# The second layer's graph-attention loop, run one step deeper

## The reference, cut to what matters

```
h = relu(layernorm(x))
score   = h @ H_v                                    # one number for each node
logits  = where(adj != 0, adj * score[None, :], -1e30)
weights = softmax(logits, axis=-1)
x = x + weights @ h
```

## Time and profile before

| | before |
|---|---|
| median of 3 runs | 1568.05 us (1566.85 to 1569.98) |
| profiled execution | 1554.0 us |
| its span | 1552.3 us |
| TensorE products, busy | 1006.1 us (65% of the span) |
| VectorE, busy | 895.8 us |
| GpSimd, busy | 768.8 us |
| ScalarE, busy | 756.1 us |
| bytes moved | 219.73 MB, 142 GB/s on average |

### The profile page before, as it was taken

The page is one execution under the profiler, slowest core; times in us unless marked ns, Lnnn a source line. Parts: engine busy times, 40 slices in busy tenths (PEclk is TensorE's granted clock), DMA queues, the critical chain, the costliest instruction groups (busy, mean ns, idle before and its releaser), DMA issues.

```text
span 1552.3 us, 29120 instructions
## 1 busy us (share of the span) xinstructions
PE 1006.1 (65%) x6426; PEld 631.8 (41%) x6426; DVE 895.8 (58%) x2430; ACT 756.1 (49%) x3228; POOL 768.8 (50%) x791
## 2 busy tenths in 40 slices
PE   4696858888974515545554286981746777777770
PEld 1353524544542314434443243441524554555440
DVE  3494855986886235544555750103436777777778
ACT  4997666678741313323333250000625666676762
POOL 3007766764555256555655505665054555555550
PEclk9797979898986556665766688996868999999995
DMA  8546656874512444554445876855242445333462
GB/s 272 194 192 227 223 182 180 257 230 166 208 40 64 122 129 101 104 100 94 109 104 98 95 245 224 301 186 62 82 134 79 106 97 105 97 105 100 101 89 58
DMA packets 124455, 219.73 MB, mean 142 GB/s; under 512 B 37350, under 2 KB 93290, under 8 KB 118762
## 3 DMA queue, kind: packets, MB, share of 16 engines
q0 software_dynamic: 25984, 60.45, 21.8%
q1 hardware_dynamic: 83050, 74.24, 15.4%
q10 hardware_dynamic: 15360, 84.43, 14.3%
HBM read 182.18 MB, written 33.18 MB: 139 GB/s over the span
## 4 chain that ended last, share of the span: by engine, by line
DVE 30%; issue 22%; PE 18%; another core or an unknown queue 13%; DVEq 6%; ACT 3%; DMA 3%; SPq 1%; ACTq 1%
DVE work L1380 4%; DVE work L1114 4%; PE ps L1673 3%; PE ps L1716 3%; DVE work L1115 2%; PE ps L1725 2%; PE ps L1526 2%; DVEq L418 1%; DVE work L1051 1%; DVE work L1048 1%; DVE work L1396 1%; DVEq L322 1%; DMA work<-adj_table 1%; PE ps L1522 1%
## 5 line engine op out<-in xcount | busy, mean ns | idle before, releaser
L685 POOL DMA_INDIRECT work<-h_table,stage x304 | 290.6, 956 | 258.8 <-issue 124.9
L801 ACT ACTIVATE unread<-work 128x128 bf16<-128x128 f32 x1024 | 301.0, 295 | 40.8 <-DVE work L1119 16.5
L685 POOL DMA_INDIRECT work<-kv_table,stage x212 | 201.5, 951 | 222.3 <-PE ps L1735 120.5
L642 POOL DMA_INDIRECT work<-in_adj_rows,adj_stage x184 | 238.4, 1296 | 82.6 <-issue 57.0
L1568 PE MATMUL ps<-work,h_wide 128*128 128x512 f32 x512 | 248.5, 641 | 25.5 <-ACT h_wide L732 18.3
L801 ACT ACTIVATION_READ_ACCUMULATOR unread<-work 128x1 f32 x1024 | 191.5, 187 | 7.3 <-issue 6.9
L1380 DVE CUSTOM_DVE_ANT_0 work<-ps,work 128x512 f32<-128x512 f32 x200 | 141.7, 748 | 76.5 <-remote 40.9
L1568 PEld LDWEIGHTS ps<-work,h_wide 128*128 128x128 f32 x512 | 103.7, 208 | 153.7 <-issue 144.8
L1725 PE MATMUL ps<-ident,work 128*128 128x128 f32 x776 | 116.9, 284 | 43.5 <-DVE work L1396 25.1
L893 ACT ACTIVATE work<-work 128x512 f32<-128x512 f32 x197 | 139.8, 713 | 3.5 <-DVE work L1389 2.9
L1648 PE MATMUL ps<-work 128*128 128x128 f32 x384 | 85.9, 394 | 68.9 <-ACT work L842 52.3
(11 more groups left out here) (216 smaller groups left out, 1802.4 us busy)
## 6 DMA issues: line engine op xcount, KB each, us to landing
work<-in_adj_rows ACTq DMA_DIRECT2D x38, 2048.0 KB
work<-adj_table SPq DMA_DIRECT2D x76, 256.0 KB
work<-in_adj_rows SPq DMA_DIRECT2D x6, 2048.0 KB
adj_table<-work SPq DMA_DIRECT2D x96, 128.0 KB
mask_table<-work SPq DMA_DIRECT2D x53, 128.0 KB
work<-mask_table SPq DMA_DIRECT2D x53, 128.0 KB
work<-h_table,stage POOLq DMA_INDIRECT x304
kv_table<-work SPq DMA_DIRECT2D x32, 128.0 KB
```

Source lines behind the costliest of these rows:

```text
L642: nc.gpsimd.indirect_dma_start(out=ag[:, h, c, :], out_offset=None, in_=adj_rows, in_offset=bass.IndirectOffsetOnAxis(ap=adj_stage[:, h // ...
L685: nc.gpsimd.indirect_dma_start(out=rows[:, b, c, :], out_offset=None, in_=table, in_offset=bass.IndirectOffsetOnAxis(ap=stage[:, b, c:c + ...
L801: ins = nc.scalar.activation(unread[:, m % (MQ // 2) * TB + t, :], ring[:, q, m, t * P:(t + 1) * P], ACT.Abs, accum_out=seen[:, b, t, q * ...
```

## The change

The loop's order is changed on three engines; no operation of a group is added or taken away.

- VectorE makes logits four groups ahead instead of two and before the maximum, takes the maximum two groups ahead instead of one, and adds up group g as before.
- The transposed logits and their source `lgT` have three buffers instead of two (PSUM banks 0, 1 and 2).
- TensorE, in step g, transposes the exponentials of g+1, multiplies those of g, and then transposes the logits of g+3.
- ScalarE, in step g, copies the transposed exponentials of g+1 and makes exponentials and mask of g+2. The copies, `eT`, have two buffers.
- The parts ahead of the loops, the waits' constants and the primed semaphores follow. SP's and GpSimd's orders stay; the semaphores that they wait for (`lgT_ready`, `mk_ready`) now come from earlier steps, and after the loop SP waits for one more mask.

```diff
--- before.py
+++ after.py
@@ -175,7 +175,7 @@
         hg2 = work[:, 2048:4096].rearrange("p (b c f) -> p b c f", b=NBUF2, c=QC)
         kvg = work[:, 0:6144].rearrange("p (b c f) -> p b c f", b=NBUF, c=QC)
         neg = work[:, 6168:6680]
-        lgT = work[:, 6680:7704].rearrange("p (b c n) -> p b c n", b=2, c=QC)
+        lgT = work[:, 6680:8216].rearrange("p (b c n) -> p b c n", b=3, c=QC)
         e = work[:, 8704:12800].rearrange("p (b h m) -> p b h m", b=2, h=H)
         e1 = e[:, :, 0, :]
         eT = work[:, 12800:14848].rearrange("p (c h n) -> p c h n", c=QC, h=H)
@@ -299,6 +299,7 @@
                   oT_out, o_done, lgT_ready, lg_done, cap_ready, eT_outd, mk_ready, mk_ready] + [mk_free] * NBUF
         for k in (1, 2, 3):
             primed += [pv_done[k], pv_done[k], pv_read[k], pv_read[k], state_reset[k]]
+        primed += [pv_read[1], pv_read[1]]
         for k in (1, 3):
             primed += [mx_ready[k], e_ready[k], e_ready[k], al_ready[k], eT_done[k], eT_out[k]]
 
@@ -540,7 +541,7 @@
                 steps = sparse_quads(sp, step) if k == 2 else each_quad(sp, step)
                 if k == 1:
                     end = Quad(steps, 0)
-                    sp.wait_ge(mk_ready, end.q + 3)
+                    sp.wait_ge(mk_ready, end.q + 4)
                     for n in range(NBUF - 1):
                         sp.dma_start(mask_table[bass.ds((end.q + n) * P, P), :], mk[:, 0, :]).then_inc(mk_all, 16)
                     sp.wait_ge(mk_all, 16 * (NBUF - 1))
@@ -827,30 +828,33 @@
                 act.wait_ge(eT_done[1], q + 1)
                 act.wait_ge(pv_read[1], q + 1)
                 nc.scalar.activation(alpha[:, b:b + 1], grown[:, b:b + 1], ACT.Exp).then_inc(al_ready[1], 1)
-                nc.scalar.activation(e1[:, b % 2, :], ps[:, b % 2, :], ACT.Exp, bias=nbest[:, b:b + 1],
+                nc.scalar.activation(e1[:, b % 2, :], ps[:, b % 3, :], ACT.Exp, bias=nbest[:, b:b + 1],
                                      accum_out=part[:, b:b + 1]).then_inc(e_ready[1], 1)
 
             def mask1(g):
 
                 act.wait_ge(mk_free, g.q + 1)
-                nc.scalar.activation(mk[:, g.b, :], ps[:, g.b % 2, :], ACT.Relu, bias=half_neg[:, 0:1],
+                nc.scalar.activation(mk[:, g.b, :], ps[:, g.b % 3, :], ACT.Relu, bias=half_neg[:, 0:1],
                                      scale=-1.0).then_inc(mk_ready, 1)
 
             def turned1(g):
                 act.wait_ge(eT_done[1], g.q + 2)
-                act.wait_ge(pv_done[1], g.q + 2)
-                nc.scalar.activation(eT[:, :, 0, :], ps[:, 3, :].rearrange("p (c n) -> p c n", c=QC),
+                act.wait_ge(pv_done[1], g.q + 1)
+                nc.scalar.activation(eT[:, :, g.b % 2, :], ps[:, 3, :].rearrange("p (c n) -> p c n", c=QC),
                                      ACT.Copy).then_inc(eT_out[1], 1)
 
             def step1(g):
-                turned1(g)
-                exps1(g.ahead(1))
-                mask1(g.ahead(1))
+                turned1(g.ahead(1))
+                exps1(g.ahead(2))
+                mask1(g.ahead(2))
 
             use_exp()
             act.wait_ge(tables_ready, 1)
             exps1(Quad(0, 0))
             mask1(Quad(0, 0))
+            turned1(Quad(0, 0))
+            exps1(Quad(0, 1))
+            mask1(Quad(0, 1))
             each_quad(act, step1)
 
             normalise(2)
@@ -1226,13 +1230,13 @@
                 adj_loaded(dve, 1, g)
                 nodes_gathered(dve, 1, g)
                 dve.wait_ge(lgT_ready, q + 1)
-                wait(dve, lg_done, q)
+                wait(dve, lg_done, q - 1)
                 link = Link(dve, link_a, 1, q)
                 link(nc.vector.tensor_scalar(neg, ac[:, b, :, :].rearrange("p c n -> p (c n)"), 0.0, NEG,
                                              ALU.is_equal, ALU.mult))
                 link.end()
                 for c in range(QC):
-                    ins = nc.vector.scalar_tensor_tensor(lgT[:, b % 2, c, :], ac[:, b, c, :], hg1[:, b, c, P:P + 1],
+                    ins = nc.vector.scalar_tensor_tensor(lgT[:, b % 3, c, :], ac[:, b, c, :], hg1[:, b, c, P:P + 1],
                                                          neg[:, c * P:(c + 1) * P], ALU.mult, ALU.add)
                 ins.then_inc(lgT_ready, 1)
 
@@ -1243,7 +1247,7 @@
                 capped = cap[:, bass.ds(q, 1)]
                 dve.wait_ge(lg_done, q + 2)
                 link = Link(dve, link_m, 2, q)
-                link(nc.vector.tensor_reduce(want, ps[:, b % 2, :], AX.X, ALU.max))
+                link(nc.vector.tensor_reduce(want, ps[:, b % 3, :], AX.X, ALU.max))
                 link(nc.vector.scalar_tensor_tensor(best[:, b:b + 1], old, capped, want, ALU.min, ALU.max))
                 link.end()
                 nc.vector.scalar_tensor_tensor(grown[:, b:b + 1], old, capped, best[:, b:b + 1], ALU.min, ALU.subtract)
@@ -1262,7 +1266,7 @@
                 settle(dve)
                 nc.vector.scalar_tensor_tensor(acc[:, t, :], acc[:, t, :], alpha[:, b:b + 1], ps[:, 4 + b % 4, 0:P], ALU.mult,
                                                ALU.add).then_inc(pv_read[1], 1)
-                dve.wait_ge(pv_read[1], q + 3)
+                dve.wait_ge(pv_read[1], q + 5)
                 settle(dve)
 
             def finish1():
@@ -1284,8 +1288,8 @@
                 link.end()
 
             def step1(g):
-                maxima(g.ahead(1))
-                logits(g.ahead(2))
+                logits(g.ahead(4))
+                maxima(g.ahead(2))
                 add_up(g)
 
             dve.wait_ge(mean_done, T + 1)
@@ -1297,11 +1301,17 @@
                                   .to_broadcast([P, T + 1, P])).then_inc(state_reset[1], 1)
             dve.wait_ge(state_reset[1], 2)
             logits(Quad(0, 0))
+            logits(Quad(0, 1))
             maxima(Quad(0, 0))
-            logits(Quad(0, 1))
+            logits(Quad(0, 2))
+            maxima(Quad(0, 1))
+            logits(Quad(0, 3))
             end = Quad(each_quad(dve, step1), 0)
 
-            dve.wait_ge(e_ready[1], end.q + 3)
+            dve.wait_ge(e_ready[1], end.q + 4)
+            dve.wait_ge(eT_out[1], end.q + 2)
+            dve.wait_ge(lg_done, end.q + 4)
+            dve.wait_ge(mk_ready, end.q + 4)
             settle(dve)
             finish1()
             dve.wait_ge(stat_done2, 1)
@@ -1628,27 +1638,37 @@
             def logits(g):
                 q, b = g.q, g.b
                 pe.wait_ge(lgT_ready, q + 2)
-                pe.wait_ge(mk_ready, q + 1)
+                wait(pe, mk_ready, q)
                 for c in range(QC):
-                    ins = nc.tensor.transpose(ps[:, b % 2, c * P:(c + 1) * P], lgT[:, b % 2, c, :], ident[:, :])
+                    ins = nc.tensor.transpose(ps[:, b % 3, c * P:(c + 1) * P], lgT[:, b % 3, c, :], ident[:, :])
                 ins.then_inc(lg_done, 1)
 
-            def step1(g):
+            def turn_exps1(g):
                 q, b = g.q, g.b
                 pe.wait_ge(e_ready[1], q + 3)
                 pe.wait_ge(eT_out[1], q + 1)
                 for c in range(QC):
                     ins = nc.tensor.transpose(ps[:, 3, c * P:(c + 1) * P], e1[:, b % 2, c * P:(c + 1) * P], ident[:, :])
                 ins.then_inc(eT_done[1], 1)
-                logits(g.ahead(1))
+
+            def weigh1(g):
+                q, b = g.q, g.b
                 pe.wait_ge(eT_out[1], q + 2)
                 pe.wait_ge(pv_read[1], q + 1)
                 nodes_gathered(pe, 1, g)
                 for c in range(QC):
-                    ins = mm(ps[:, 4 + b % 4, 0:P], eT[:, c, 0, :], hg1[:, b, c, 0:P], start=(c == 0), stop=(c == QC - 1))
+                    ins = mm(ps[:, 4 + b % 4, 0:P], eT[:, c, b % 2, :], hg1[:, b, c, 0:P], start=(c == 0), stop=(c == QC - 1))
                 ins.then_inc(pv_done[1], 1)
 
+            def step1(g):
+                turn_exps1(g.ahead(1))
+                weigh1(g)
+                logits(g.ahead(3))
+
             logits(Quad(0, 0))
+            logits(Quad(0, 1))
+            turn_exps1(Quad(0, 0))
+            logits(Quad(0, 2))
             each_quad(pe, step1)
 
             project(2)
```

## The result

The changed kernel takes 1587.82 us (median of 4 runs, 1582.98 to 1589.87), the kernel before beside it 1569.01 us. The ratio is 1.0113, 95% interval 1.0081 to 1.0145: slower by 1.1%, 18.8 us between the medians. Forecast was 1556.3 us and faster. The time lies inside the range given, on the side of the slower rival, but far from that rival's 1603 us.

What follows compares the result with a forecast made beforehand. The second layer's loop was taken as bound by a two-group cycle of gathers and held TensorE results, 12.3 us. SP's queue -10.1, Start +4.7 and End -6.4 sum to -11.8: 1568.05 becomes 1556.3 us; whole range 1536 to 1598.

Steps and rivals of the forecast that it cites:

- slower rival: Second layer's loop: gathers come too late, pace 7.28 us a step, +35.3 us with the start, 1603 us; chance 0.30.
- End: After the second layer's loop: SP reaches its last masks and lists one step earlier, third layer's first gather too; -6.4 us.
- DMA path to 942.06: After the loop: from SP's 2 MB loads at 896.04 us to the third layer's first gather at 942.06.
- The gathers' slack: Loop: logits two steps earlier leave gathers two steps of four; costs 0, with 2.4 us to spare over three steps.
- The ring of 16.0 us: Loop: gather, landing, logits, maximum, exponential, transposes, sums, to the next gather; 16.0 us for three steps, 5.3 a step.
- The pattern of 7.28 us a group: Fourth layer's loop, where one group is gathered and then waited for; the slower rival takes its 7.28 us as pace.
- SP's queue: Loop: logits and mask come earlier, so GpSimd's waits for SP's loads shrink from 19.7 us to 0; -10.1 us.
- no change: Loop: GpSimd's permission and cycle stay, SP's gain returns as longer holds, or held time is TensorE's; 1568 us, chance 0.16.
- Start: Loop's start: group 0's sums now also stand behind the weights of group 1; +4.7 us.
- Signals: Loop: longer distance from logits' transposes to maximum; two groups still get through per run of gathers; 0.
- much faster: Loop: late results have a cause independent of gathers, depth hides holds, 5.0 us a step; 1515 us, chance 0.12.

Runs made afterwards that it cites:

- e13: Kernel before with unused list places naming 128 different rows instead of one, on a chip of the second kind: 1335.82 us, ratio 0.9896.
- e14: Changed kernel with unused list places naming 128 different rows instead of one, on a chip of the second kind: ratio 1.0016.
- e9: Kernel before with the second layer's indirect gathers replaced by plain DMAs of 128 consecutive rows, on a chip of the first kind: 1477.61 us, ratio 0.9425.
- e12: Changed kernel with logits three groups ahead, behind the maximum, on a chip of the second kind: 1356.94 us, ratio 1.0067.
- e19: Changed kernel with logits three groups ahead, behind the maximum, and unused list places naming 128 different rows, on a chip of the first kind: ratio 1.0037.
- e15: Changed kernel with logits three groups ahead, behind the maximum, and unused list places naming 128 different rows, on a chip of the second kind: ratio 0.9977.
- e16: Changed kernel, unaltered, on a chip of the second kind: 1382.02 us, ratio 1.0251 to the kernel before.
- e2: Changed kernel with logits three groups ahead, behind the maximum, on a chip of the first kind: ratio 0.9972.

## Why the prediction was wrong

**End: the step that failed.** The prediction put the two more groups of logits "at the loop's end, beside the DMA path to 942.06", where they "cost nothing while that path ends last". The loads did go out earlier, by less than the 6.4 us taken: from the first gather to their issue it is 340.7 us in the mean of three profiles, against 344.2. It bought nothing, because that path did not end last. In all profiles with gathers, on both kinds of chip, the third layer's first gather comes 64.8 to 65.9 us after the last addition, while from the loads to that gather it is anything from 45.1 to 62.0 us. The prediction had named this among its signs of being wrong ("if what follows the loop waits for VectorE's longer tail rather than for DMA") and priced it at +3.4 us. And those logits aren't 3.4 us of VectorE's time: they wait for the gathers of spare groups, which land about 7 us apart. The last five steps cost +10.5 us, where the term had -6.4.

**The gathers' slack failed at the same place.** The ring of 16.0 us took 3.3 us for the landing, read from the loop's first group in the earlier trace rows. In the tail the logits start 6.8 us after the last issue, which makes the ring 19.5 us, 6.5 a step, before any hold. The slower rival named the sign, "VectorE's L1231 waits for gathers in most steps" (17, 13 and 12 of 36 in the middle of three profiles, so not in most; but each one at the end). The pattern of 7.28 us a group was reached in the last five steps, 35.8 us, and not in the 36 of the middle, which is why the time lies short of 1603 us.

**SP's queue** was right in its cause and wrong in its size. The waits vanished (0.6 us), the pace gained 3.2 us over 36 steps instead of 10.1. A part of the 10.1 was the one profile that it was read from: 6.43 us a step there, 6.36 in the mean of three. The prediction's warning, that what SP gains is returned as holds, held: GpSimd's waits for late releases grew by 19.6 us. To that extent the rival "no change" was right about the middle.

**Start.** +4.7 was forecast; it is +0.5 at the first addition and +4.0 at the seventh; what adds the 3.5 between them wasn't looked into. On these chips the first addition comes only after GpSimd's first run of six groups is over, at 34.0 to 34.9 us in every profile, with or without the change. On chips without holds the same edit costs 12.2 us (18.9 in e13 to 31.1 in e14): the first addition stands behind the logits of group 4 instead of group 2, two gathers of 5.0 us later. That makes 10.0; the other 2.2 us aren't placed.

**Signals** were taken as 0. Their part can't be told from that of SP's queue, since the pace shows only the sum; copies still wait 53.2 us for remote. **The rival "much faster"** rested on late results having a cause apart from gathers; e9 excludes that on chips of the first kind. It also excludes that the held time is TensorE's own, the other reading under "no change". The rule of the Trainium skill quoted in the prediction (SBUF — State Buffer, who interferes with whom) would let one expect no such holds; on chips of the first kind the traces show them (the copies' 53.2 us), though not where they arise, and on chips of the second kind the trace of e12 has none.

**Open:** how much of the +10.5 us on the first kind of chip is the slow gathers and how much the held releases. The changed kernel's logits wait for gathers in each of the last five steps of its profile above, but e19 shows that with fast gathers the holds take their place, and the changed kernel with spread rows was not run there.

## What to carry to other kernels

Where gathers set the pace, work that looks n groups ahead and stands in an in-order queue ahead of the result delays that result by n gathers: count it in gathers, not in its own instructions. With even gathers it is paid once: two, three and four groups ahead (e13, e15, e14) differ at the first addition, 18.9, 23.9 and 31.1 us, and not in the last five steps, 25.4, 25.1 and 24.6 us. The end cost extra where the spare groups' gathers were slow (e16, 37.0 us). Before taking a tail for free, find what the next stage really starts from; here one subtraction over several profiles (last addition to next gather, always 65 us) says it. Let the padding of an index list name different rows, not one; it gave 1.0% on chips of the second kind and nothing measurable on those of the first.

## What the hardware showed

- Gathers whose indices all name one row are slow: 0.52 us a packet in e16, 0.59 in the kernel before (845 to 890 us: 60.9% of 16 engines for 744 packets), against 0.13 to 0.14 with 128 different rows (e14, e19). A spare group's logits then start 5 to 7 us after its last issue (e16, changed kernel) instead of 2.5 (e14).
- Chips of one type differ. On some, TensorE's releases are held while GpSimd issues indirect gathers, and the first addition is at 34 to 35 us, whatever the order; on others nothing is held (e12), and the same kernel takes 1348 instead of 1560 us. The first layer is shorter there too (first gather at 497 to 501 instead of 547 to 561 us), and the stretch from the fourth layer's first gather to the end takes 344 to 346 instead of 416 to 425 us, which isn't explained. The same kernel, e2 and e12, was level with the kernel before on one kind (0.9972 [0.994, 1.001]) and 0.7% slower on the other.
- Plain DMAs from the same queue hold nothing back (e9: no wait for remote from 618 to 850 us).
